# Three steps moved in the hand-written order of an attention and expert kernel: transposed maxima, low query parts and values

## The chip, the cores and the metric

The kernel runs on one core of a Trainium2 chip. Its time is the device time of one launch in microseconds (us). The core has five engines that run side by side, each strictly in the order of its own program: TensorE (PE, with its weight loads PEld), VectorE (DVE), ScalarE (ACT), GpSimd (POOL) and SyncE (SP), which here only issues DMAs. They wait for one another by semaphores. "The profiled execution" is one execution whose instructions were recorded; its span is the time from the first to the last recorded instruction.

## The reference

Eight batches of 128 rows with 256 columns go through one attention (8 heads of 16 rows, attending over the 256 columns) and one layer with two experts. Each has a layer norm ahead and a residual sum behind.

```python
def _L0_xcond_ref(q, k, v, k_length):
    qh = q.reshape(b, NUM_HEADS, d, lq)
    kh = k.reshape(b, NUM_HEADS, d, lk)
    vh = v.reshape(b, NUM_HEADS, d, lk)
    s = SCALE * jnp.log(k_length.astype(jnp.float32))[:, None, None, None]
    attn = jnp.einsum('bhdq,bhdk->bhqk', qh, kh)
    attn = jax.nn.softmax(s * attn, axis=-1)
    out = jnp.einsum('bhqk,bhdk->bhdq', attn, vh)
    return out.reshape(b, hd, lq)
...
h = jnp.einsum('nd,ehd->enh', x_flat, w_fc)
a = jnp.square(jnp.where(h >= 0, h, 0.5 * h))
expert_out = jnp.einsum('enh,edh->end', a, w_proj)
mask = (top_idx[None, :] == jnp.arange(num_experts)[:, None]).astype(x.dtype)
out = jnp.einsum('end,en->nd', expert_out, mask * top_weight[None, :])
...
x = x + _L0_xcond_ref(_layernorm(x, axis=-1), ctx_2048, ctx_2048, itok_B_779_1933)
x = x + _L0_ffn_ref(_layernorm(x, axis=-1), L0_ffn_w_router, L0_ffn_w_fc, L0_ffn_w_proj)
```

## The kernel before

Everything stays on the chip between input and output. A batch b goes through the attention alone; two batches together form a group g for the experts. Operands of the matmuls are held as a high part and a low part (q_hi and q_lo, k_hi and k_lo, and so on for the weights), the low part being the value less the high part. For queries, ScalarE makes the high part (q_part_hi) and VectorE the low one (q_part_lo, line 698). For keys, ScalarE makes the high part (k_part_hi) and GpSimd the low one (split_k, line 301).

The steps of one batch, by the names of the helpers:

- SP stacks the parts of keys and queries by six DMAs (stack_k, stack_q, lines 161 and 169) into k_st and q_st, of which there are two each, for even and odd batches. The stacks of batch b may be overwritten once all four scores_kq of batch b-2 are done.
- scores_qk(b, g), line 1141, g from 0 to 3: PE's score products for a pair of heads, from which only the row maxima are taken. The first of a batch waits for all six stacking DMAs. In batches 0 and 1 they alternate between the PSUM tiles snp and hp; from batch 2 on all go to snp, so scores_qk(b, g) also waits for row_max(b, g-1).
- row_max(b, g), line 721: VectorE's maximum over a row, negated, into negm. split_max_hi(b) and split_max_lo(b), lines 729 and 734, make the two parts nm_r of it.
- max_transpose(b), line 1156: PE transposes nm_r into snp. ScalarE copies it to mx (max_rows, line 428).
- scores_kq(b, g), lines 1171 and 1175: the scores again, transposed, with the maximum already taken off, into stp (in batch 1 into hp for even g). The first of a batch waits for mx.
- exp(b, g), line 435: ScalarE's exponential into the tile probs of pair g. It overwrites what values(b-1, 0) reads for g = 0 and 1, and what values(b-1, 1) reads for g = 2 and 3, and waits for them.
- values(b, 0) and values(b, 1), line 1191: PE's 16 matmuls each over the pairs 0 and 1, and 2 and 3, into the two halves of the PSUM tile pv.
- pv_turn(b), line 740, waits for both halves. Behind it on VectorE come den_inverse (744), attention_out (749, the division), attention_turn (755, the second transpose), x2_sum (761, the residual sum) and the statistics x2_moments (660, 663, 666).

Each pair of batches then goes through x_transpose, ffn1 (line 1213), leaky and square steps and ffn2 (line 1231). The weights of the experts come in 16 pieces by DMA and are split into parts by ScalarE with GpSimd (split_w, line 312) or VectorE. fill(n), line 1148, and warm are matmuls on a zero tile that nobody reads.

No scheduler sets the order. Each engine's program is a list of such calls, written out by hand, and the change edits two of the five lists: VectorE's and PE's.

Of the kernel before, what the change touches and what calls it, by code (L numbers as in the profile page):

```python
# [24 lines left out]
def build(nc, x, ctx_kv, ctx_t, w_router, w_fc_t, w_proj_t, consts, out):  # L25
# [3 lines left out]
    with ExitStack() as stack:  # L29
# [100 lines left out]
        def wait(eng, s, value):  # L130

            if value > 0:
                eng.wait_ge(s, value)
# [523 lines left out]
        def _(dve):  # L657
# [25 lines left out]
            def x_newton(b, stage):  # L683
                j = b % 2
                newton(stage, b, xvar[j], xrs[j], xn1[j], xsc[j], s_xrs, s_xn1, s_xsc)
# [8 lines left out]
            def q_part_lo(b):  # L694
                j = b % 2
                dve.wait_ge(s_qhi, b + 1)
                wait(dve, s_qst[j], 48 * (b // 2))
                dve.tensor_tensor(q_lo[j][:, :], q_f[j][:, :], q_hi[j][:, :].bitcast(f32), ALU.subtract).then_inc(s_qlo, 1)
# [19 lines left out]
            def row_max(b, g):  # L718
                pair = hp if b < 2 and g % 2 == 1 else snp
                dve.wait_ge(s_sn, PAIRS * b + g + 1)  # L720
                dve.tensor_reduce(negm[b % 2][:, :, :, g].rearrange("p c e -> p e c"),  # L721
                                  pair[:, :, :].rearrange("p e (c n) -> p e c n", c=KC),
                                  AX.X, ALU.max, negate=True).then_inc(s_max, 1)
# [160 lines left out]
            row_max(1, 0)  # L884
            row_max(1, 1)
            row_max(1, 2)
            row_max(1, 3)
            x_newton(3, 0)
            x_moments(4, 0)
# [2 lines left out]
            split_max_lo(1)  # L892
            x_moments(4, 2)
            x_newton(3, 1)
            q_part_lo(2)
            x_newton(4, 0)
            q_normalise(3)
            x_newton(4, 1)
# [230 lines left out]
        def _(pe):  # L1129
            def scores_qk(b, g):  # L1130
                j = b % 2
                pair, sets = (hp if b < 2 and g % 2 == 1 else snp), (2 if b < 2 else 1)
                if g == 0:
                    pe.wait_ge(s_qst[j], 48 * (b // 2) + 48)
                    pe.wait_ge(s_kst[j], 48 * (b // 2) + 48)
                    wait(pe, s_mrows, b)
                wait(pe, s_max, PAIRS * b + (g - sets + 1))
                for qc in range(KC):
                    for e in range(2):
                        rows = slice(HALF * e, HALF * e + HALF)  # L1140
                        last = pe.matmul(pair[:, e, qc * KEYS:(qc + 1) * KEYS], q_st[j][rows, g, qc * P:(qc + 1) * P],  # L1141
                                         k_st[j][rows, g, :], start=(qc == 0), stop=True, skip_group_check=True)
                last.then_inc(s_sn, 1)

            def fill(n):

                for _ in range(n):
                    pe.matmul(ops_[:, 0:P], blank[:, 0:P], blank[:, 0:P], start=True, stop=True, skip_group_check=True)

            def max_transpose(b):  # L1150
                j = b % 2
                pe.wait_ge(s_nmlo, b + 1)
                if b == 0:
                    pe.wait_ge(s_cst, 16)
                for qc in range(KC):
                    last = pe.transpose(snp[:, 0, qc * P:(qc + 1) * P],
                                        nm_r[j][:, qc, :, :].rearrange("p e r -> p (e r)").bitcast(f32), ident)
                last.then_inc(s_mt, 1)

            def scores_kq(b, g):  # L1160
                j = b % 2
                if g == 0:
                    pe.wait_ge(s_mrows, b + 1)
                    if b == 0:
                        pe.wait_ge(s_picks, 1)
                pair = hp if b == 1 and g % 2 == 0 else stp
                wait(pe, s_exp, PAIRS * b + g - (1 if b == 1 and g > 0 else 0))
                for kc in range(KC):
                    for e in range(2):
                        rows = slice(HALF * e, HALF * e + HALF)  # L1170
                        pe.matmul(pair[:, e, kc * DIM:(kc + 1) * DIM], k_st[j][rows, g, kc * P:(kc + 1) * P], q_st[j][rows, g, :],  # L1171
                                  start=(kc == 0), stop=False, skip_group_check=True)
                    for e in range(2):
                        rows = slice(HALF * e, HALF * e + HALF)
                        last = pe.matmul(pair[:, e, kc * DIM:(kc + 1) * DIM], pick[rows, g, :], mx[j][rows, :],  # L1175
                                         start=False, stop=True, skip_group_check=True)
                last.then_inc(s_st, 1)

            def values(b, e):
                j = b % 2  # L1180
                pe.wait_ge(s_exp, PAIRS * b + PAIRS // 2 * (e + 1))
                if e == 0:
                    pe.wait_ge(s_vone, b + 1)
                    if b == 0:
                        pe.wait_ge(s_vones, 2)
                    wait(pe, s_pvt, b)
                    wait(pe, s_xtlo, b // 2)
                for kc in range(KC):
                    for g in range(PAIRS):
                        h = PAIRS * e + g  # L1190
                        last = pe.matmul(pv[32 * g:32 * g + 32, e * DIM:(e + 1) * DIM], v_one[j][:, kc * HEADS + h, :],  # L1191
                                         probs[h // 2][:, h % 2, kc, :], start=(e == 0 and kc == 0), stop=(e == 1 and kc == KC - 1),
                                         skip_group_check=True)
                last.then_inc(s_pv, 1)
# [75 lines left out]
            scores_qk(1, 3)  # L1270
            fill(2)
            scores_kq(0, 3)
            values(0, 0)
            max_transpose(1)
            values(0, 1)
            scores_kq(1, 0)
            scores_kq(1, 1)
            scores_qk(2, 0)
            scores_kq(1, 2)
            values(1, 0)  # L1280
# [233 lines left out]
```

## Time and profile before

| what | us |
|---|---|
| median of 3 runs | 178.3 |
| lowest and highest run | 178.22, 179.01 |
| the profiled execution's own time | 178.59 |
| its span | 176.8 |
| PE busy (matmuls) | 160.6 |
| VectorE busy | 125.6 |
| ScalarE busy | 95.4 |
| GpSimd busy | 57.9 |

The profiled execution's time is 1.8 us above its span, and 0.3 us above the median. Busy times of different engines lie beside one another and don't add up to the span. The timelines below give, for each instruction or run of like instructions, its start in us from the beginning of the span and its duration; a bracket behind a row tells how long the engine stood idle before it, and what ended that.

### The profile page before, as it was taken

The numbers are of one execution on the slowest core, as the hardware profiler recorded it, in microseconds if no ns is written. First come the engines' busy times: TensorE is split into PE (matmuls) and PEld (weight loads), VectorE is DVE, ScalarE is ACT, GpSimd is POOL, SyncE is SP. The second block draws the span as 40 slices with busy tenths as digits, with TensorE's granted clock in tenths as the row PEclk, the third lists the DMA queues.
The fourth block names the chain that finished last, engine by engine and source line by source line (L and its number), as shares of the span: only waits on it lengthen the run. The fifth ranks groups of instructions, "written<-read, shape, count | busy, mean of one in ns | idle before, by whom it ended". The sixth has DMA issues, their size and how long they took to land.

```text
span 176.8 us, 4088 instructions
## 1 busy us (share of the span) xinstructions
PE 160.6 (91%) x1516; PEld 139.6 (79%) x1516; DVE 125.6 (71%) x298; ACT 95.4 (54%) x179; POOL 57.9 (33%) x66
## 2 busy tenths in 40 slices
PE   2987795858999999999999999999999999999990
PEld 2866653546698968869898899969879999999990
DVE  6778879988997887799969937669238449345311
ACT  4432868946566749773559353644782463434400
POOL 7232805600044922133344241202241606343310
PEclk9999999999999999999999999999999999999999
DMA  4887856672356045024000460000010000010001
GB/s 134 266 287 232 267 193 212 215 235 65 124 154 200 4 140 186 6 75 132 4 2 30 153 178 0 4 0 6 0 36 27 0 0 0 4 59 0 4 0 59
DMA packets 18355, 16.32 MB, mean 92 GB/s; under 512 B 1696, under 2 KB 18208, under 8 KB 18336
## 3 DMA queue, kind: packets, MB, share of 16 engines
q1 hardware_dynamic: 17472, 15.21, 26.9%
q10 hardware_dynamic: 864, 0.86, 1.7%
q8 instruction: 12, 0.20, 0.5%
q14 instruction: 7, 0.06, 0.1%
HBM read 8.72 MB, written 1.05 MB: 55 GB/s over the span
## 4 chain that ended last, share of the span: by engine, by line
PE 73%; DMA 7%; DVE 6%; SPq 5%; ACT 4%; issue 3%; ACTq 0%; DVEq 0%
PE ops L1231 27%; PE hp L1213 24%; PE pv L1191 6%; PE stp L1171 6%; PE snp L1141 4%; DMA q_st<-q_lo 4%; PE stp L1175 4%; DVE negm L721 3%; ACT probs L435 3%; SPq L161 2%; DMA x_raw<-x 2%; DMA q_st<-q_hi 2%; SPq L169 1%; DVE wproj_lo L841 1%; PE pv L1241 1%
## 5 line engine op out<-in xcount | busy, mean ns | idle before, releaser
L319 POOL TENSOR_TENSOR a_buf<-l_buf 128x512 f32<-128x512 f32 x32 | 35.1, 1101 | 85.6 <-ACT l_buf L443 64.0
L435 ACT ACTIVATE probs<-stp,scale_b 128x1024 f32<-128x1024 f32 x30 | 33.4, 1114 | 21.5 <-PE stp L1175 21.2
L721 DVE TENSOR_REDUCE negm<-snp 128x4 f32<-128x1024 f32 x28 | 34.2, 1223 | 13.9 <-PE snp L1141 13.6
L1213 PE MATMUL hp<-xt_hi,wfc_hi 128*128 128x256 f32 x128 | 37.5, 293 | 0.0
L1213 PE MATMUL hp<-xt_hi,wfc_lo 128*128 128x256 f32 x128 | 35.8, 279 | 0.0
L1213 PE MATMUL hp<-xt_lo,wfc_hi 128*128 128x256 f32 x128 | 35.8, 279 | 0.0
L819 DVE TENSOR_TENSOR a_lo<-a_buf,a_hi 128x512 fp32r<-128x512 f32 x32 | 23.5, 745 | 12.7 <-ACT a_hi L450 8.1
L443 ACT ACTIVATE l_buf<-hp 128x512 f32<-128x512 f32 x32 | 18.8, 593 | 17.8 <-PE hp L1213 17.8
L1231 PE MATMUL ops<-wproj_hi,a_hi 128*128 128x256 f32 x128 | 27.0, 292 | 0.0
L1213 PEld LDWEIGHTS hp<-xt_hi,wfc_hi 128*128 128x128 f32 x128 | 24.1, 188 | 2.9 <-issue 1.6
L1231 PE MATMUL ops<-wproj_hi,a_lo 128*128 128x256 f32 x128 | 25.6, 281 | 0.0
L1231 PE MATMUL ops<-wproj_lo,a_hi 128*128 128x256 f32 x128 | 25.5, 281 | 0.0
L1213 PEld LDWEIGHTS hp<-xt_hi,wfc_lo 128*128 128x128 f32 x128 | 24.1, 188 | 0.0
L1213 PEld LDWEIGHTS hp<-xt_lo,wfc_hi 128*128 128x128 f32 x128 | 24.1, 188 | 0.0
L450 ACT ACTIVATE a_hi<-l_buf 128x512 fp32r<-128x512 f32 x32 | 19.7, 625 | 3.8 <-PE ops L1231 3.7
L1231 PEld LDWEIGHTS ops<-wproj_hi,a_hi 128*128 128x128 f32 x128 | 19.5, 188 | 1.7 <-issue 0.4
L1171 PE MATMUL stp<-q_st,k_st 64*128 64x256 f32 x120 | 17.6, 313 | 3.1 <-ACT probs L435 2.1
L1231 PEld LDWEIGHTS ops<-wproj_lo,a_hi 128*128 128x128 f32 x128 | 19.6, 188 | 0.0
L1231 PEld LDWEIGHTS ops<-wproj_hi,a_lo 128*128 128x128 f32 x128 | 19.6, 188 | 0.0
L1141 PE MATMUL snp<-k_st,q_st 64*128 64x256 f32 x112 | 12.9, 309 | 4.4 <-DMA q_st<-q_lo 3.2
L1191 PE MATMUL pv<-probs,v_one 128*32 128x256 f32 x256 | 16.2, 384 | 0.3 <-DVE xt_lo L846 0.3
L1171 PEld LDWEIGHTS stp<-q_st,k_st 64*128 64x128 f32 x120 | 11.2, 184 | 6.3 <-ACT probs L435 3.1
(81 smaller groups left out, 224.9 us busy)
## 6 DMA issues: line engine op xcount, KB each, us to landing
k_st<-k_hi SPq DMA_DIRECT2D x16, 128.0 KB, 2.5
wfc_raw<-w_fc_t SPq DMA_DIRECT2D x8, 256.0 KB, 3.6
wproj_raw<-w_proj_t SPq DMA_DIRECT2D x8, 256.0 KB, 3.2
q_st<-q_hi SPq DMA_DIRECT2D x14, 128.0 KB, 2.4
x_raw<-x SPq DMA_DIRECT2D x8, 128.0 KB, 2.6
v_raw<-ctx_t SPq DMA_DIRECT2D x8, 128.0 KB, 2.8
k_st<-k_lo SPq DMA_DIRECT2D x8, 128.0 KB, 2.5
q_st<-q_lo SPq DMA_DIRECT2D x8, 128.0 KB, 2.3
```

What stands on the lines that cost most here:

```text
L319: pool.tensor_tensor(a_buf[d % 2][:, :, :], l_buf[d % 2][:, :, :], l_buf[d % 2][:, :, :], ALU.mult).then_inc(s_a, 1)
L435: act.activation(probs[g][:, :, :, :], (hp if b == 1 and g % 2 == 0 else stp)[:, :, :].rearrange("p e (c n) -> p e c n", c=KC), ACT.Exp, s ...
L443: act.activation(l_buf[d % 2][:, :, :], hp[:, d % 2, :].rearrange("p (c n) -> p c n", c=2), ACT.Prelu, alpha=0.5).then_inc(s_l, 1)
L450: act.activation(a_hi[d % NA][:, :, :], l_buf[d % 2][:, :, :], ACT.Square).then_inc(s_ahi, 1)
L721: dve.tensor_reduce(negm[b % 2][:, :, :, g].rearrange("p c e -> p e c"), pair[:, :, :].rearrange("p e (c n) -> p e c n", c=KC), AX.X, ALU. ...
L819: dve.tensor_tensor(a_lo[d % NA][:, :, :], a_buf[d % 2][:, :, :], a_hi[d % NA][:, :, :].bitcast(f32), ALU.subtract).then_inc(s_alo, 1)
L1141: last = pe.matmul(pair[:, e, qc * KEYS:(qc + 1) * KEYS], q_st[j][rows, g, qc * P:(qc + 1) * P], k_st[j][rows, g, :], start=(qc == 0), sto ...
L1171: pe.matmul(pair[:, e, kc * DIM:(kc + 1) * DIM], k_st[j][rows, g, kc * P:(kc + 1) * P], q_st[j][rows, g, :], start=(kc == 0), stop=False, ...
L1175: last = pe.matmul(pair[:, e, kc * DIM:(kc + 1) * DIM], pick[rows, g, :], mx[j][rows, :], start=False, stop=True, skip_group_check=True)
L1191: last = pe.matmul(pv[32 * g:32 * g + 32, e * DIM:(e + 1) * DIM], v_one[j][:, kc * HEADS + h, :], probs[h // 2][:, h % 2, kc, :], start=(e ...
L1213: last = pe.matmul(hp[:, d % 2, half], wfc[w][:, kc, c * P:(c + 1) * P], xt[:, kc, :], start=(c % 2 == 0 and kc == 0 and w == 0 and xt is ...
L1231: last = pe.matmul(ops_[:, t * DIM:(t + 1) * DIM], a[d % NA][:, c % 2, t * P:(t + 1) * P], wproj[w][:, c, :], start=(c % CH == 0 and part ...
```

## The change

```diff
@@ -884,6 +884,7 @@
             row_max(1, 0)
             row_max(1, 1)
             row_max(1, 2)
+            q_part_lo(2)
             row_max(1, 3)
...
             split_max_lo(1)
             x_moments(4, 2)
             x_newton(3, 1)
-            q_part_lo(2)
             x_newton(4, 0)
@@ -1270,11 +1270,11 @@
             scores_kq(0, 3)
+            max_transpose(1)
             values(0, 0)
-            max_transpose(1)
-            values(0, 1)
             scores_kq(1, 0)
             scores_kq(1, 1)
+            values(0, 1)
             scores_qk(2, 0)
```

On VectorE, the low query parts of batch 2 are made ahead of the last maximum of batch 1 instead of seven rows behind it. On PE, the transposed maxima of batch 1 go ahead of the first half of batch 0's values, and the second half of these values goes behind the first two transposed score products of batch 1. No instruction is added or removed, and the programs of ScalarE, GpSimd and SP are as before.

PE's order before, from the end of scores_kq(0, 3) to the first score product of batch 2; pv is the tile of the values, the row into snp from nm_r is max_transpose(1), hp and stp take scores_kq(1, 0) and (1, 1):

```order
L1175 MATMUL stp<-mx,pick 128x256 x2
L1191 MATMUL pv<-probs,v_one 32x256 x8
L1156 MATMUL snp<-cst,nm_r 128x128 x2
L1191 MATMUL pv<-probs,v_one 32x256 x8
L1171 MATMUL hp<-q_st,k_st 128x256 x2
L1175 MATMUL hp<-mx,pick 128x256 x2
...
L1171 MATMUL stp<-q_st,k_st 128x256 x2
L1175 MATMUL stp<-mx,pick 128x256 x2
L1141 MATMUL snp<-k_st,q_st 128x256 x4
```

The same stretch in the changed kernel:

```order
L1175 MATMUL stp<-mx,pick 128x256 x2
L1156 MATMUL snp<-cst,nm_r 128x128 x2
L1191 MATMUL pv<-probs,v_one 32x256 x8
L1171 MATMUL hp<-q_st,k_st 128x256 x2
L1175 MATMUL hp<-mx,pick 128x256 x2
...
L1171 MATMUL stp<-q_st,k_st 128x256 x2
L1175 MATMUL stp<-mx,pick 128x256 x2
L1191 MATMUL pv<-probs,v_one 32x256 x8
L1141 MATMUL snp<-k_st,q_st 128x256 x4
```

The transposes have passed the first half of the values, and the second half now stands directly ahead of batch 2's first score product.

VectorE's order in the changed kernel as a difference to before, with buffer numbers; negm1 takes batch 1's maxima and q_lo0 batch 2's low query parts:

```order
 L721 TENSOR_REDUCE negm1<-hp 128x2x2
 L721 TENSOR_REDUCE negm1<-snp 128x2x2
+L698 TENSOR_TENSOR q_lo0<-q_f0,q_hi0 128x256
 L721 TENSOR_REDUCE negm1<-hp 128x2x2
 L672 SCALAR_TENSOR_TENSOR xn11<-xrs1,xvar1 128x1
...
 L666 TENSOR_SCALAR xvar0<-xmv0 128x1
 L675 SCALAR_TENSOR_TENSOR xsc1<-xn11,xrs1 128x1
-L698 TENSOR_TENSOR q_lo0<-q_f0,q_hi0 128x256
 L672 SCALAR_TENSOR_TENSOR xn10<-xrs0,xvar0 128x1
 L691 TENSOR_SCALAR q_f1<-x_raw1,xmv1,xsc1 128x256
```

The subtraction has passed row_max(1, 3), the two split steps of the maxima and four small statistics.

What follows on VectorE stands in the same order before and after, from pv_turn(0), which reads pv, to row_max(2, 0), which reads snp:

```order
L740 STREAM_TRANSPOSE pvt<-pv 128x512
L744 RECIPROCAL den_r<-pvt 128x16
L749 TENSOR_TENSOR att_t<-pvt,den_r 128x2x128
L755 STREAM_TRANSPOSE att<-att_t 128x256
L698 TENSOR_TENSOR q_lo1<-q_f1,q_hi1 128x256
L761 TENSOR_TENSOR x2_0<-x_keep0,att 128x256
L660 BN_STATS yst0<-x2_0 128x6
L663 BN_AGGR ymv0<-yst0 128x2
L721 TENSOR_REDUCE negm0<-snp 128x2x2
```

Nothing in this chain was moved; its first step waits for values(0, 1), which was.

## Rows read from the trace of the kernel before

**Rows 1.** The page, part 1: busy us (share of the span) xinstructions.

```profile
PE 160.6 (91%) x1516; PEld 139.6 (79%) x1516; DVE 125.6 (71%) x298; ACT 95.4 (54%) x179; POOL 57.9 (33%) x66
```

**Rows 2.** PE's waits, 53 to 177 us: us in total, times, longest.

```profile
PE snp L1141 <- DMA q_st<-q_lo: 0.2, 1, 0.2
```

**Rows 3.** PE's timeline, 20 to 34 us: start, duration, what, [idle before].

```profile
23.37 1.07 PE L1191 MATMUL pv<-probs,v_one 128*32 128x256 f32 x16
24.37 0.44 PE L1156 MATMUL snp<-cst,nm_r 128*128 128x128 f32 x2
24.74 1.07 PE L1191 MATMUL pv<-probs,v_one 128*32 128x256 f32 x16
25.74 0.39 PE L1171 MATMUL hp<-q_st,k_st 64*128 64x256 f32 x2
...
26.68 0.28 PE L1175 MATMUL stp<-mx,pick 64*128 64x256 f32 x2
28.97 0.51 PE L1141 MATMUL snp<-k_st,q_st 64*128 64x256 f32 x4 [2.01 <-DMA q_st<-q_lo]
...
30.87 0.50 PE L1141 MATMUL snp<-k_st,q_st 64*128 64x256 f32 x4
```

**Rows 4.** The timeline of SP's DMA issues, 20 to 34 us.

```profile
24.93 0.54 SPq L161 DMA_DIRECT2D k_st<-k_hi  x1
...
26.86 0.55 SPq L169 DMA_DIRECT2D q_st<-q_lo  x1
...
32.63 1.47 SPq L161 DMA_DIRECT2D k_st<-k_hi  x1
```

**Rows 5.** ScalarE's timeline, 20 to 34 us.

```profile
20.90 0.41 ACT L402 ACTIVATE q_hi<-q_f 128x256 fp32r<-128x256 f32 x1
...
24.85 0.38 ACT L428 ACTIVATE mx<-snp 128x256 fp32r<-128x256 f32 x1
...
27.85 0.42 ACT L396 ACTIVATE k_hi<-kv_raw 128x256 fp32r<-128x256 f32 x1
```

**Rows 6.** VectorE's timeline, 20 to 34 us.

```profile
21.77 1.23 DVE L721 TENSOR_REDUCE negm<-hp 128x4 f32<-128x1024 f32 x1 [0.40 <-PE hp L1141]
...
23.59 0.15 DVE L734 TENSOR_TENSOR nm_r<-negm,nm_r 128x16 fp32r<-128x16 f32 x1
...
25.88 0.72 DVE L740 STREAM_TRANSPOSE pvt<-pv 128x512 f32<-128x512 f32 x1 [0.31 <-PE pv L1191]
...
26.92 0.43 DVE L749 TENSOR_TENSOR att_t<-pvt,den_r 128x256 f32<-128x256 f32 x1
27.38 0.45 DVE L755 STREAM_TRANSPOSE att<-att_t 128x256 f32<-128x256 f32 x1
27.98 0.42 DVE L698 TENSOR_TENSOR q_lo<-q_f,q_hi 128x256 fp32r<-128x256 f32 x1 [0.15 <-ACT q_hi L402]
...
29.23 0.18 DVE L663 BATCH_NORM_AGGREGATE ymv<-yst 128x2 f32<-128x6 f32 x1
29.52 1.23 DVE L721 TENSOR_REDUCE negm<-snp 128x4 f32<-128x1024 f32 x1
```

**Rows 7.** GpSimd's timeline, 20 to 34 us.

```profile
21.08 0.74 POOL L301 TENSOR_TENSOR k_lo<-kv_raw,k_hi 128x256 fp32r<-128x256 f32 x1
28.34 0.98 POOL L301 TENSOR_TENSOR k_lo<-kv_raw,k_hi 128x256 fp32r<-128x256 f32 x1 [6.53 <-ACT k_hi L396]
29.29 1.28 POOL L312 TENSOR_TENSOR wfc_lo<-wfc_raw,wfc_hi 128x512 fp32r<-128x512 f32 x1
```

**Rows 8.** VectorE's timeline, 93 to 97 us.

```profile
95.32 0.76 DVE L698 TENSOR_TENSOR q_lo<-q_f,q_hi 128x256 fp32r<-128x256 f32 x1
```

**Rows 9.** GpSimd's timeline, 93 to 97 us.

```profile
94.75 1.04 POOL L319 TENSOR_TENSOR a_buf<-l_buf 128x512 f32<-128x512 f32 x1 [2.86 <-ACT l_buf L443]
95.75 0.92 POOL L301 TENSOR_TENSOR k_lo<-kv_raw,k_hi 128x256 fp32r<-128x256 f32 x1
```

**Rows 10.** DMAs issued 24.9 to 25.0 us: KB, us from issue to landing.

```profile
k_st<-k_hi SPq DMA_DIRECT2D x1, 128.0 KB, 2.8
```

## The prediction

> **What bounds the kernel now.** I read the page's busy shares, then PE's waits by stretch, then the timelines of all engines between 20 and 34 us. The page says that PE is busy for 91% of the span, and that VectorE (DVE) comes next at 71% [rows 1]. PE's waits over the last 124 us, from 53 us on, are one wait of 0.2 us [rows 2]. So from 53 us PE works without a pause, and a delay of PE before that point is a delay of the end: nothing later can take it up. All three moved pieces lie between 21 and 26 us, in the stage in which PE still waits. There the reader is to look at two waits of PE. The first score product of batch 2, scores_qk(2, 0), starts at 28.97 after 2.01 us of idle time, released by a DMA (the low query parts of batch 2). The next one, scores_qk(2, 1), starts at 30.87, right behind the values of batch 1 [rows 3].
>
> The 28.97 is fixed from elsewhere. SP's queue issues six stacking DMAs for batch 2, one after another, the third at 24.93 and the last at 26.86 [rows 4]. They may start only when scores_kq(0, 3) is done, which the change doesn't move, and the last of them lands about 2.1 us after its issue. Anything on PE between 23.4 and 28.97 can be reordered without moving that product. What can move is the work behind it that VectorE has to do in time.
>
> **Part 1, the low query parts of batch 2 ahead of a maximum.** q_part_lo(2) needs the high parts, which ScalarE has ready at 20.90 + 0.41 = 21.31 [rows 5]. VectorE is idle for 0.40 us before row_max(1, 3), which starts at 21.77 [rows 6]. The piece takes 0.42 (as q_part_lo(3) does at 27.98, same rows), so it would run from 21.33 to 21.75 and cost nothing. But GpSimd runs k_lo, a subtraction of two SBUF tiles, from 21.08 to 21.82 [rows 7]. Late in the kernel the same meeting is on record: q_lo started at 95.32, 0.57 us into a GpSimd operation of 1.04 us from 94.75, and took 0.76 in place of 0.42. It ended 0.29 after that operation's end, and the GpSimd operation behind it took 0.92 in place of 0.74 [rows 8, 9]. By that, q_part_lo(2) ends at 21.82 + 0.29 = 22.11 and row_max(1, 3) starts some 0.25 us late. I take 0.25, with 0 as the other end. What this piece brings is nothing: its DMA stands last in SP's series and goes at 26.86, long after either time.
>
> **Part 2, the transposed maxima ahead of values(0, 0).** Before, max_transpose(1) starts at 24.37, after 1.00 us of values work that began at 23.37 [rows 3]. After, it waits for split_max_lo(1), whose last step was done at 23.59 + 0.15 = 23.74 [rows 6] and is now done at about 24.0. The transposes start at 24.05, and values(0, 0) at 24.05 + 0.37 = 24.42, with its next work 1.00 later, at 25.42. ScalarE copies the maxima at 24.85 in either case, since it comes from exp(0, 3) and two small steps that end then [rows 5]; the copy is done at 25.23. So scores_kq(1, 0) starts at 25.42 in place of 25.74. This is a gain of 0.3 us for exp(1, 0), and of 0.5 without the 0.25 of part 1. It is lost again: exp(1, 2) has to wait for a product that stands behind scores_qk(2, 0) at 28.97 on PE.
>
> **Part 3, values(0, 1) behind two score products.** It started at 24.74 and now starts after scores_kq(1, 0) and (1, 1), whose matmuls run from 25.74 to the last pair at 26.68 [rows 3]. Other work can start about 0.2 behind that pair, so they hold PE for 1.15, and 25.42 + 1.15 = 26.57. It ends at 27.64 in place of 25.81. On PE that is still free, since PE then idles until 28.97. On VectorE it isn't. pv_turn(0), the transpose that reads both halves of the values, started at 25.88, right behind them [rows 6], and now starts at 27.71, 1.83 later. Behind it, in program order, stand the inverse, the division (26.92), the second transpose (27.38), q_part_lo(3) (27.98), x2_sum(0), two moment steps (the last at 29.23, 0.18 long, so done at 29.41), and only then row_max(2, 0) at 29.52. The last of these frees the score bank for scores_qk(2, 1). Before, this chain ended 0.1 us before the scores came: the slack is used up.
>
> Without any meeting with GpSimd: VectorE is free for q_part_lo(3) 1.95 us after pv_turn started (27.38 + 0.45 - 25.88), at 29.66 (or 29.48 without the 0.25 of part 1). From q_lo's start to the end of the moments it takes 29.41 - 27.98 = 1.43, so row_max(2, 0) starts at about 31.0, ends at 32.2, and scores_qk(2, 1) starts at 32.25 in place of 30.87. That is 1.4 late, or 1.2 without the 0.25. I call this 1.3.
>
> **What the shifted chain runs into.** GpSimd runs k_lo(4) at 28.34 and right behind it a weight split of 1.28 us from 29.29 [rows 7]. Before, VectorE was done with its operations on two SBUF tiles when the split began, and only k_lo(4) was touched (0.98, where k_lo at 21.08 took 0.74). These don't move with the change: k_lo(4) waits for ScalarE's k_hi(4) at 27.85 [rows 5], and that needs the batch-2 stacking DMA issued at 24.93, which lands 2.8 us later, at 27.7 [rows 4, 10]. So GpSimd now holds 28.34 to 29.08 and, behind it, 1.28 us more. VectorE comes to the division at 27.71 + 1.04 = 28.75, inside k_lo(4), and ends it at 29.08 + 0.29 = 29.37. Its second transpose goes to 29.83. Meanwhile the weight split has begun, held up by 0.18 as in [rows 9], and ends at 29.05 + 1.28 + 0.18 = 30.5. q_part_lo(3) reaches the engine at 29.74 and ends 0.29 after the split, at 30.8. The rest of the chain takes 29.41 - 28.40 = 1.01, so row_max(2, 0) starts at about 31.8, ends at 33.0, and scores_qk(2, 1) starts at 33.0: 33.0 - 30.87 = **2.1 us late**. The 0.25 of part 1 drops out here, because GpSimd's end sets the time.
>
> The Trainium skill (SBUF — State Buffer, section "Who interferes with whom") says that a VectorE instruction with two SBUF inputs and a GpSimd instruction that reads SBUF exclude each other for a whole instruction, and whichever was issued first holds the ports. The trace agrees where it shows the meeting, with 0.76 in place of 0.42 [rows 8]. By this rule the delay is the 2.1; if it did not hold for the pairs met here, it would be the 1.3.
>
> **Does the delay travel?** scores_kq(1, 3) stands right behind scores_qk(2, 1), and its end releases batch 3's stacking DMAs, whose landing releases scores_qk(3, 0). The other maxima of batch 2 follow one another through PE and VectorE, each product behind the maximum before it. Both paths shift whole. The one thing that could give back is SP's issue at 32.63, which took 1.47 where its like took 0.54 to 0.59 [rows 4]. If the stall behind that is over by the time SP comes there, up to 0.9 is regained on the DMA path, though the path by the exponentials would keep most of the delay. I take 0 and keep 0.9 for the range.
>
> **The sum.** Part 1 gives 0, part 2 gives 0, and part 3 costs 2.1, of which 1.3 is program order and 0.8 is the meeting with GpSimd. The profiled execution took 178.59 with a span of 176.8, so it would take 180.7. The median of the runs is 178.3, 0.3 lower, and on it I predict **180.4 us**, 1.2% more.
>
> **The rivals.**
> First, GpSimd costs nothing, because the division or q_part_lo(3) slips ahead of the weight split: 1.3 late, 179.6. For it speaks that single times here are within 0.1 to 0.2 us of each other; against it, that q_part_lo(3) falls into the middle of a 1.28 us operation. Chance 0.17.
> Second, the delay is made up before 53 us (SP's 0.9 and shorter landings once the weight loads are through): 0 to 0.6 late, 178.3 to 178.9. Against it speak the waits on maxima and on exponentials that shift as well. Chance 0.09.
> Third, faster: the 0.3 to 0.5 us by which scores_kq(1, 0) comes earlier is handed on, 177.8. It would need the chain behind pv_turn(0) to be done by 29.52, that is, values(0, 1) done by about 25.9, or VectorE to need less than the 3.53 us that it took from 25.88 to 29.41. Work that was back to back has no such room. Chance 0.04.
> Fourth, still slower: another meeting with GpSimd, whose weight splits go on, or a DMA stall that now falls worse. Over 181.0, chance 0.10.
> The forecast itself, 1.6 to 2.6 late, has 0.60.
>
> **How the numbers follow.** Leaving out the second and third rival and the fourth leaves out 0.23. To come under 0.2 the range goes from 179.2 (the first rival with some of SP's 0.9 given back) to 181.1. A measurement of this kernel can tell about 0.5%, 0.9 us, from no change. Slower by more than that are the forecast, the fourth rival and nearly all of the first: 0.85. Within it are most of the second and a little of the first: 0.11. Faster: 0.04.
>
> **What would show it.** In the profile after, scores_qk(2, 0) should stand at about 29.0 as before, scores_kq(1, 0) at 25.2 to 25.5, pv_turn(0) at 27.5 to 27.7, q_part_lo(3) at 29.5 to 29.8 with a duration near 1.0, row_max(2, 0) at 31.8, and scores_qk(2, 1) at 33.0 after an idle time of about 2 us that a maximum ends. q_part_lo(2) should take about 0.75. Batch 3's first product should be 1.2 to 2.1 later. I am wrong if scores_qk(2, 0) moves, if q_part_lo(3) takes 0.42, or if PE's start on the first expert product isn't later by what scores_qk(2, 1) was.

## The result, and the profile after

The changed kernel took 182.1 us (median of 4 runs, 181.7 to 183.9), the kernel before 178.6 beside it. The ratio is 1.018, with a 95% interval of 1.013 to 1.024. The sign was right; the size was forecast at 2.1 us and is 3.5, and 182.1 lies above the predicted range of 179.2 to 181.1. Ratios here and below leave out runs that lie more than 1.5% above the fastest of their kernel. The profiled execution took 182.02 with a span of 180.2, 3.4 more than before. Each run also lists TensorE's mean granted clock as a share of full speed. Here it was 0.966 to 0.991 and never full, and that will matter.

The page's parts 1 and 2 of the kernel after (PEclk is the granted clock of 40 slices, in tenths):

```profile
PE 162.9 (90%) x1516; PEld 140.7 (78%) x1516; DVE 126.8 (70%) x298; ACT 95.4 (53%) x179; POOL 57.7 (32%) x66
PEclk9999999969999999999999999999999999999998
```

The same 1516 matmuls are busy for 2.3 us longer than in [rows 1], and one slice, 36.0 to 40.6 us, has a 6 where before had 9 throughout. So TensorE waited longer and, for a moment, also worked slower.

PE's waits of the kernel after, 20 to 36 us (us in total, times, longest):

```profile
PE snp L1141 <- DVE negm L721: 2.5, 2, 2.3
PE snp L1141 <- DMA q_st<-q_lo: 1.3, 1, 1.3
```

The timeline of PE, same kernel (start, duration, what, idle before and its releaser), with max_transpose(1), the moved values(0, 1), scores_qk(2, 0) and scores_qk(2, 1). It answers to [rows 3]:

```profile
24.26 0.44 PE L1156 MATMUL snp<-cst,nm_r 128*128 128x128 f32 x2 [0.58 <-DVE nm_r L734]
...
25.63 0.39 PE L1171 MATMUL hp<-q_st,k_st 64*128 64x256 f32 x2
...
26.79 1.07 PE L1191 MATMUL pv<-probs,v_one 128*32 128x256 f32 x16
29.16 0.50 PE L1141 MATMUL snp<-k_st,q_st 64*128 64x256 f32 x4 [1.30 <-DMA q_st<-q_lo]
...
33.43 0.51 PE L1141 MATMUL snp<-k_st,q_st 64*128 64x256 f32 x4 [2.30 <-DVE negm L721]
```

The new wait is the one that was forecast: scores_qk(2, 1) idles 2.30 us for a maximum and starts at 33.43. All records of this execution lie about 0.2 later from 21 us on (scores_qk(2, 0) too), so net of that it is 2.4 late.

The timelines of VectorE and GpSimd, same kernel. They answer to [rows 6, 7]: q_part_lo(2), then the chain from pv_turn(0) to row_max(2, 0), then GpSimd's k_lo(4) and the weight split:

```profile
21.57 0.76 DVE L698 TENSOR_TENSOR q_lo<-q_f,q_hi 128x256 fp32r<-128x256 f32 x1
...
27.93 0.72 DVE L740 STREAM_TRANSPOSE pvt<-pv 128x512 f32<-128x512 f32 x1 [2.12 <-PE pv L1191]
28.68 0.25 DVE L744 RECIPROCAL den_r<-pvt 128x16 f32<-128x16 f32 x1
28.96 1.51 DVE L749 TENSOR_TENSOR att_t<-pvt,den_r 128x256 f32<-128x256 f32 x1
30.50 0.45 DVE L755 STREAM_TRANSPOSE att<-att_t 128x256 f32<-128x256 f32 x1
30.87 0.38 DVE L698 TENSOR_TENSOR q_lo<-q_f,q_hi 128x256 fp32r<-128x256 f32 x1
...
32.19 1.19 DVE L721 TENSOR_REDUCE negm<-snp 128x4 f32<-128x1024 f32 x1
```

```profile
28.22 0.72 POOL L301 TENSOR_TENSOR k_lo<-kv_raw,k_hi 128x256 fp32r<-128x256 f32 x1 [6.17 <-ACT k_hi L396]
28.90 1.28 POOL L312 TENSOR_TENSOR wfc_lo<-wfc_raw,wfc_hi 128x512 fp32r<-128x512 f32 x1
```

The meeting with GpSimd is there, in another place. The division comes at 28.96, just behind the end of k_lo(4) (28.22 + 0.72 = 28.94) and 0.06 us into the weight split, and waits for the split's end: 28.90 + 1.28 + 0.29 = 30.47, where it ends. It takes 1.51 in place of the 0.43 or so that it takes undisturbed, and q_part_lo(3) finds the way free with 0.38. The forecast had the division come inside k_lo(4). But k_lo(4) starts at 28.22 in place of 28.34, which is 0.3 earlier net of the 0.2: on ScalarE, exp(1, 0) starts at 26.42 in place of 26.52, and k_hi(4) follows it.

The windows of the kernel after (busy us of PE, PEld, DVE, ACT, POOL with counts, then the granted clock, DMA share, GB/s):

```profile
32.00:33.00 1.00, 0.00 (x0) 0.00 (x0) 0.97 (x3) 0.00 (x0) 1.00 (x1) 1.00 0.32 102
...
35.00:36.00 1.00, 0.80 (x9) 0.52 (x12) 0.48 (x5) 1.00 (x4) 0.00 (x0) 0.70 0.23 75
36.00:37.00 1.00, 1.00 (x12) 0.48 (x16) 1.00 (x1) 1.00 (x3) 0.44 (x1) 0.50 0.24 65
37.00:38.00 1.00, 1.00 (x10) 0.25 (x4) 0.34 (x2) 1.00 (x4) 0.83 (x1) 0.50 0.61 204
38.00:39.00 1.00, 1.00 (x7) 0.78 (x8) 1.00 (x2) 0.32 (x3) 0.00 (x0) 0.59 0.67 211
```

This is the other cost. TensorE does nothing from 31.13 to 33.43 and then works at the full clock (2.4 GHz) until about 35.4. From there to about 38.8 it has half of it (1.2 GHz), and then the full one again. Before, the windows from 33 to 39 us all show 1.00. The Trainium skill (TensorE: Matmul & The Clock Gate, section "Part 1: The HAM clock gate") says that the clock follows how busy TensorE has been shortly before; the trace agrees in that the half clock follows the idle time, though it doesn't come in it.

The work in the stretch at half the clock is on the way to the end. PE's timeline, the kernel before and then the kernel after: values(1, 1), max_transpose(2), scores_qk(3, 0), and the first expert product:

```profile
33.12 1.07 PE L1191 MATMUL pv<-probs,v_one 128*32 128x256 f32 x16
...
36.76 0.44 PE L1156 MATMUL snp<-cst,nm_r 128*128 128x128 f32 x2 [0.43 <-DVE nm_r L734]
...
39.79 0.50 PE L1141 MATMUL snp<-k_st,q_st 64*128 64x256 f32 x4 [0.96 <-DMA q_st<-q_lo]
...
47.52 0.39 PE L1213 MATMUL hp<-xt_hi,wfc_hi 128*128 128x256 f32 x1
```

```profile
35.88 1.93 PE L1191 MATMUL pv<-probs,v_one 128*32 128x256 f32 x16
...
40.29 0.44 PE L1156 MATMUL snp<-cst,nm_r 128*128 128x128 f32 x2 [0.28 <-DVE nm_r L734]
...
42.29 0.50 PE L1141 MATMUL snp<-k_st,q_st 64*128 64x256 f32 x4
...
50.66 0.39 PE L1213 MATMUL hp<-xt_hi,wfc_hi 128*128 128x256 f32 x1
```

values(1, 1) takes 1.93 in place of 1.07. As a sum of what the traces show:

| start of | before | after | later | of it |
|---|---|---|---|---|
| scores_qk(2, 0) | 28.97 | 29.16 | 0.2 | start of the trace |
| scores_qk(2, 1) | 30.87 | 33.43 | 2.6 | 2.4 for the maximum |
| max_transpose(2) | 36.76 | 40.29 | 3.5 | 1.0 more at half the clock |
| scores_qk(3, 0) | 39.79 | 42.29 | 2.5 | its DMA was waited for 0.96 before, 0 now |
| scores_kq(2, 1) | 40.13 | 43.15 | 3.0 | waits for an exponential of batch 2 |
| first expert product | 47.52 | 50.66 | 3.1 | |
| scores_qk(4, 0) | 53.16 | 56.60 | 3.4 | its DMA was waited for 0.24 before, 0.55 now |

Batch 3's first product gives 1.0 back, but the chain of batch 2 (maximum, transposed maximum, exponential) gives back only 0.5, and the end follows that one. The last 0.3 comes at batch 4's first product. PE's rows before and after, and SP's issue ahead of it in the kernel after, where the same issue before took 1.57:

```profile
53.16 0.50 PE L1141 MATMUL snp<-k_st,q_st 64*128 64x256 f32 x4 [0.24 <-DMA q_st<-q_lo]
```

```profile
56.60 0.51 PE L1141 MATMUL snp<-k_st,q_st 64*128 64x256 f32 x4 [0.55 <-DMA q_st<-q_lo]
```

```profile
51.07 1.80 SPq L177 DMA_DIRECT2D v_raw<-ctx_t  x1
```

From 57 us on PE doesn't wait at all.

### The profile page after: what moved, and what is told of

Read it like the earlier page. It is cut to its first block, busy times and chain, and to the rows that moved or that the text cites. A ratio compares the mean times of both kernels' runs of the same rounds, so it can differ in the third digit from the quotient of the medians.

```text
span 180.2 us, 4088 instructions
## 1 busy us (share of the span) xinstructions
PE 162.9 (90%) x1516; PEld 140.7 (78%) x1516; DVE 126.8 (70%) x298; ACT 95.4 (53%) x179; POOL 57.7 (32%) x66
## 3 DMA queue, kind: packets, MB, share of 16 engines
q1 hardware_dynamic: 17472, 15.21, 26.5%
HBM read 8.72 MB, written 1.05 MB: 54 GB/s over the span
## 4 chain that ended last, share of the span: by engine, by line
PE 77%; DVE 12%; issue 4%; ACT 4%; DMA 1%; DVEq 0%; ACTq 0%
PE ops L1231 26%; PE hp L1213 24%; PE pv L1191 8%; PE stp L1171 6%; DVE negm L721 5%; PE snp L1141 4%; PE ops L1200 4%; PE stp L1175 3%; ACT probs L435 2%; DMA q_st<-q_lo 1%; PE snp L1156 1%; DVE wproj_lo L841 1%; DVE q_st L713 1%; PE pv L1241 1%; DVE att_t L749 1%
## 5 line engine op out<-in xcount | busy, mean ns | idle before, releaser
L450 ACT ACTIVATE a_hi<-l_buf 128x512 fp32r<-128x512 f32 x32 | 19.7, 625 | 3.8 <-PE ops L1231 3.7
L1191 PE MATMUL pv<-probs,v_one 128*32 128x256 f32 x256 | 17.1, 399 | 0.3 <-DVE xt_lo L846 0.3
```

Of the source, the lines that this page charges most:

```text
L450: act.activation(a_hi[d % NA][:, :, :], l_buf[d % 2][:, :, :], ACT.Square).then_inc(s_ahi, 1)
```

## The experiments

My theory after the result had three parts. (a) values(0, 1) behind the score products carries the whole loss. (b) Of it, 1.3 is program order on VectorE and about 1 the meeting with GpSimd. (c) The idle time of TensorE brings a stretch at half the clock, worth about 1.3 more. The rivals: the moved query parts delay everything (against a), and the rest comes from a DMA or maximum path and not from the clock (against c). In what follows "at the full clock" means runs whose mean granted clock was 0.995 or more. There the kernel before took 178.5 to 179.0 (medians of 6, 8 and 6 such runs on three chips, of 55 in all).

**PE's two moves without the query parts.** The changed kernel, with q_part_lo(2) back in its place.

```diff
             row_max(1, 2)
-            q_part_lo(2)
             row_max(1, 3)
```

> The two moves on PE alone (transposed maxima ahead of values(0, 0), values(0, 1) behind two score products); VectorE's order as before. Theory: all of the loss is PE's two moves, by three terms that follow one another: the chain on VectorE behind values(0, 1), the division that waits for GpSimd, and half the TensorE clock after PE's long idle time. Then scores_qk(2, 1) stands at 33.2 to 33.5 as in the changed kernel and the time is 181.7 to 182.3. Rival: the low query parts ahead of the maximum, which took 0.76 in place of 0.42 there, carry a good part of it; then this is under 181.2.

Measured: 183.2 to 184.4 (4 runs), ratio 1.026 [1.021, 1.031]. The loss stays, so the query parts don't cause it. It is larger than I expected, because the clock was also at half from 20 to 26 us in the profiled execution, before any of the moves could act. The profiled executions of the next two experiments, which carry no loss, show the same early fall; the one profile of the kernel before doesn't. The three lines are the window, the division and scores_qk(2, 1):

```profile
24.00:26.00 2.00, 2.00 (x12) 1.56 (x11) 2.00 (x9) 1.03 (x2) 0.00 (x0) 0.50 0.44 141
```

```profile
31.23 1.52 DVE L749 TENSOR_TENSOR att_t<-pvt,den_r 128x256 f32<-128x256 f32 x1
```

```profile
35.72 0.50 PE L1141 MATMUL snp<-k_st,q_st 64*128 64x256 f32 x4 [2.17 <-DVE negm L721]
```

**The query parts alone.** The kernel before, with q_part_lo(2) ahead of row_max(1, 3) and nothing else.

> The low query parts of batch 2 ahead of row_max(1, 3) alone, PE's order as before. Theory: q_part_lo(2) takes 0.76 beside GpSimd's subtraction and row_max(1, 3) starts 0.25 late, but the transposed maxima stand behind values(0, 0) on PE until 24.4 anyway: 178.3 to 178.9, no difference. Rival: it costs by itself what it delays, 0.3 us, or sets off something later: 179.2 or more.

Measured: 178.5 to 179.1 in the four runs at the full clock, ratio 1.0025 [0.997, 1.008]. No difference; its own duration was 0.76, as in the changed kernel. The profiled execution (182.4) has the early fall, and a second one behind the 1.91 us that PE waits for the low query parts: half the clock from 33.2 to 36.6. So the wait that the kernel before has already can be followed by one too.

**The transposed maxima alone.** The kernel before with max_transpose(1) ahead of values(0, 0), and values(0, 1) behind it as before.

```diff
+            max_transpose(1)
             values(0, 0)
-            max_transpose(1)
             values(0, 1)
```

> The kernel before with one edit: the transposed maxima of batch 1 ahead of both halves of batch 0's values, which stay together; the low query parts stay. Theory: harmless. The transposes wait 0.4 us, values(0, 1) ends within 0.4 us of where it did (26.0 to 26.2), row_max(2, 0) within 0.4 of 29.5, and runs at full clock take 178.3 to 178.9. Rival, that the transposes' wait is part of the loss: 179.2 or more at full clock.

Measured: 178.1 to 179.2 in the six runs at the full clock, 0.996 [0.992, 1.000]. Harmless.

**The values alone.** The kernel before with only values(0, 1) moved.

```diff
-            values(0, 1)
             scores_kq(1, 0)
             scores_kq(1, 1)
+            values(0, 1)
             scores_qk(2, 0)
```

> The kernel before with one edit: values(0, 1) behind scores_kq(1, 0) and (1, 1); the transposed maxima stay between the two halves of the values, the low query parts stay where they were. Theory: this one move carries the loss. values(0, 1) is done about 1.2 us later than before and the division meets GpSimd's k_lo(4) and weight split as in the changed kernel: scores_qk(2, 1) at 32.5 to 33.5, time 181 to 182.5. Rival, that the loss needs the transposes ahead too: under 180.

Measured: 181.4 to 182.3 (4 runs, clock 0.987 to 0.991), 1.014 [1.008, 1.020]. This one line is the loss. The division, scores_qk(2, 1), what PE waits for before the clock falls, and the window of the fall:

```profile
28.93 1.50 DVE L749 TENSOR_TENSOR att_t<-pvt,den_r 128x256 f32<-128x256 f32 x1
```

```profile
33.40 0.50 PE L1141 MATMUL snp<-k_st,q_st 64*128 64x256 f32 x4 [2.19 <-DVE negm L721]
```

```profile
39.30 0.44 PE L1156 MATMUL snp<-cst,nm_r 128*128 128x128 f32 x2 [0.43 <-DVE nm_r L734]
40.21 0.39 PE L1171 MATMUL stp<-q_st,k_st 64*128 64x256 f32 x2 [0.47 <-ACT mx L428]
...
41.90 0.50 PE L1141 MATMUL snp<-k_st,q_st 64*128 64x256 f32 x4 [0.53 <-DMA q_st<-q_lo]
```

```profile
42.00:44.00 2.00, 2.00 (x16) 1.78 (x17) 1.56 (x3) 1.25 (x4) 0.40 (x1) 0.63 0.51 142
```

Here the clock stays full until about 42.5 and falls then, 9 us behind the end of the wait. Right ahead of this fall TensorE had three short idle times, 0.43, 0.47 and 0.53. The kernel before has the same ones at 36.3 to 39.8 (0.43, 0.47, 0.96) and keeps the full clock behind them in its profile. So this trace doesn't tell which idle time the fall belongs to.

**The gap filled.** TensorE's idle time before scores_qk(2, 1) is filled with products of a blank tile that nobody reads (fill, which the kernel has in other gaps already).

```diff
             values(1, 0)
+            fill(16)
             scores_qk(2, 1)
```

> The changed kernel with 16 matmuls on the zero tile between values(1, 0) and scores_qk(2, 1), about 1.9 us of work that nobody reads, in PE's idle time of 2.3. Nothing is left out. Theory: scores_qk(2, 1) stays at 33.4, the granted clock stays full between 35 and 40 us, where it is at half in the changed kernel, and the time is 0.8 to 1.2 lower: 180.9 to 181.3. Rival, that the clock falls for another reason or costs nothing: 182.0 to 182.3, half clock still seen.

Measured: 183.2 median, ratio 1.023 [1.014, 1.032], and 182.0 and 182.1 in the two runs at the full clock. I had the size of a fill wrong: fill(16) is 32 matmuls and takes 3.84 us.

```profile
31.16 3.84 PE L1148 MATMUL ops<-blank 128*128 128x128 f32 x32
34.93 0.50 PE L1141 MATMUL snp<-k_st,q_st 64*128 64x256 f32 x4
```

That makes scores_qk(2, 1) some 1.4 later than it need be. Repeated with fill(9), 2.27 us:

> The changed kernel with 9 fill steps (18 matmuls on the zero tile, 2.2 us) between values(1, 0) and scores_qk(2, 1), so that they fit PE's idle time of 2.3 (16 such steps took 3.84 us and were too many). Nothing is left out. Theory: scores_qk(2, 1) stays at 33.4, the clock stays full from 35 to 40 us, and runs whose clock is at 0.995 or more take 180.7 to 181.2, against 181.7 to 182.2 for the changed kernel. Rival, that the half clock there has nothing to do with the idle time: it is seen between 35 and 39 us all the same and the time is 181.7 or more.

Measured: five of ten runs at the full clock, and these took 180.5 to 180.7; the others 181.7 to 183.9, down to a clock of 0.966 (ratio 1.011 [1.006, 1.016]). I had expected 180.7 to 181.2 at the full clock. The distance between scores_qk(2, 0) and (2, 1) is 4.13 in this trace and 4.27 in that of the changed kernel, so the fill delays nothing. The wait is as long as before, only busy: I take 180.6 for the changed kernel without its half clock. Its stretch behind the gap, with the clock full:

```profile
36.00:38.00 2.00, 1.75 (x20) 1.41 (x20) 1.90 (x6) 1.17 (x2) 0.02 (x1) 1.00 0.49 144
```

**The same fill without the query parts** (the first experiment with fill(9)):

> PE's two moves alone, the low query parts where they were, with 9 fill steps ahead of scores_qk(2, 1). Nothing is left out. Theory: the low query parts ahead of the maximum cost nothing beside PE's moves, since GpSimd's split sets the time: runs at full clock take 180.3 to 180.7, as the changed kernel does with the same fill steps. Rival, that they cost their 0.25 us: 180.1 to 180.3. A third, that they matter more: under 180.

Measured: 180.4 to 180.7 in the five of ten runs at the full clock; ratio 1.012 [1.008, 1.017]. That is 0.2 below the runs with them, but on another chip, and between these two chips the kernel before differs by 0.5 (178.5 and 179.0). Whether the query parts cost 0 or their 0.25 isn't shown.

**The maximum first.** The changed kernel with row_max(2, 0) directly behind den_inverse(0), ahead of the division and all that follows.

```diff
             den_inverse(0)
+            row_max(2, 0)
             attention_out(0)
...
             x2_moments(0, 1)
-            row_max(2, 0)
```

> The changed kernel, with row_max(2, 0) on VectorE put directly behind the inverse, ahead of the division, second transpose, low query parts, residual sum and moments. Nothing is left out. Theory: scores_qk(2, 1) waits for VectorE's program order; row_max(2, 0) then runs at 29.7 (right behind the scores), scores_qk(2, 1) starts at 31.0 to 31.2, PE's idle time ahead of it is gone, and the time is that of the kernel before within 0.8 us: 178.4 to 179.5 where the clock stays full. Rival, that the late end of the values costs by another way (a tile that comes free late, a DMA): 180.5 or more.

Measured: 183.9 median, 1.026 [1.020, 1.033]. A clear miss. scores_qk(2, 1) starts at 31.36 without a wait, as wanted, and the wait reappears one product on, longer:

```profile
31.36 0.51 PE L1141 MATMUL snp<-k_st,q_st 64*128 64x256 f32 x4
...
36.43 0.79 PE L1141 MATMUL snp<-k_st,q_st 64*128 64x256 f32 x4 [3.44 <-DVE negm L721]
```

The chain that I had moved out of the way now stands in front of row_max(2, 1), where its residual sum meets the next weight split:

```profile
32.43 1.49 DVE L761 TENSOR_TENSOR x<-x_keep,att 128x256 f32<-128x256 f32 x1
...
35.16 1.21 DVE L721 TENSOR_REDUCE negm<-snp 128x4 f32<-128x1024 f32 x1
```

VectorE has the same work to do between values(0, 1) and batch 2's second maximum, wherever the first one stands. This change of the order within it freed no time.

**The weight split out of the way.** Three tries at (b), each the changed kernel with GpSimd's split moved. First, split 3 ahead of k_lo(4):

```diff
             split_k(3)
-            split_k(4)
             split_w(0, 3)
+            split_k(4)
```

> The changed kernel, with GpSimd's fourth weight split put ahead of its k_lo(4) (it can run from 23.2 us on, where GpSimd is idle). Nothing is left out. This takes the operation away into which VectorE's division runs. Theory: the division takes 0.43 in place of 1.51, scores_qk(2, 1) starts 1.1 earlier, at about 32.3, PE's idle time ahead of it is 1.2 and the clock stays full: 179.6 to 180.2. If the clock falls all the same: 180.6 to 181.2. Rival, that GpSimd isn't the cause of the 1.51: 182.

Measured: 183.0 median, 1.013 [1.006, 1.020]. The division took 0.43, but the moved split now met the steps that prepare the transposed maxima (a cast took 1.16), and in the profiled execution the clock fell three times, at 19.7, 26.5 and 36.7. Not conclusive. With a fill(4) before scores_qk(2, 1):

> The changed kernel with GpSimd's fourth weight split ahead of k_lo(4), so that the division no longer meets it, and 4 fill steps (1 us) ahead of scores_qk(2, 1) for the clock. Nothing is left out. Theory: the division takes 0.43, scores_qk(2, 1) starts at 32.2 to 32.5 and what is left is the cost of program order alone, 1.3 us: 179.6 to 180.2 where the clock stays full. Rival, that GpSimd's part was small: 180.7 or more.

Measured: 181.7 median, 1.012 [1.002, 1.021]; 180.4 and 180.7 at the full clock. No gain over 180.6, against what I expected. The rows of VectorE and GpSimd show why:

```profile
23.74 1.28 POOL L312 TENSOR_TENSOR wfc_lo<-wfc_raw,wfc_hi 128x512 fp32r<-128x512 f32 x1 [1.43 <-ACT wfc_hi L463]
24.14 0.91 DVE L729 CAST nm_r<-negm 128x16 fp32r<-128x16 f32 x1
```

A cast of 16 columns takes 0.91 in place of 0.15. What the division saves, the transposed maxima lose. Last, the split later instead: GpSimd holds split 3 until ScalarE has the next piece's high parts.

```diff
-                pool.wait_ge(s_whi[w], n + 1)
+                pool.wait_ge(s_whi[w], n + 2 if w == 0 and n == 3 else n + 1)
```

> The changed kernel with GpSimd's fourth weight split made to wait for the high parts of the fifth piece, so that it starts at about 31.8, behind VectorE's operations with two SBUF inputs, and 4 fill steps ahead of scores_qk(2, 1). Nothing is left out. Theory: the division takes 0.43, scores_qk(2, 1) starts at 32.2 to 32.4 in place of 33.4, and runs at full clock take 179.3 to 179.9, against 180.5 to 180.7 for the changed kernel with its idle time filled. Rival, that GpSimd's hold on the division isn't worth 1 us to the end: 180.3 or more.

Measured: 179.95 and 181.17 at the full clock, both above what I expected; median 181.7, 1.011 [1.004, 1.018]. In the trace the first half of (b) stands bare: the division undisturbed, and scores_qk(2, 1) 3.22 behind scores_qk(2, 0), where it was 1.90 [rows 3]. The 1.32 is program order alone.

```profile
28.89 0.42 DVE L749 TENSOR_TENSOR att_t<-pvt,den_r 128x256 f32<-128x256 f32 x1
```

```profile
29.06 0.50 PE L1141 MATMUL snp<-k_st,q_st 64*128 64x256 f32 x4 [1.28 <-DMA q_st<-q_lo]
...
32.28 0.50 PE L1141 MATMUL snp<-k_st,q_st 64*128 64x256 f32 x4 [0.16 <-DVE negm L721]
...
34.72 0.50 PE L1141 MATMUL snp<-k_st,q_st 64*128 64x256 f32 x4 [0.82 <-DVE negm L721]
```

But the late splits, two in a row, then held a piece of batch 4's queries for 1.06 in place of 0.41, and scores_qk(2, 2) waited for it with 0.82. A meeting was moved again, not removed. In this trace the clock is at half from 42 to 48 us, in spite of the fill.

**Fills for the kernel before.** If idle time costs clock, the kernel before should gain as well where it waits. It gets 11 more fills: one more behind scores_qk(0, 3), one behind max_transpose(0), two ahead of scores_kq(0, 1), and seven ahead of scores_qk(2, 0):

```diff
             scores_kq(1, 1)
+            fill(7)
             scores_qk(2, 0)
```

> The kernel before with matmuls on the zero tile in PE's idle times: 2 fill steps more around the transposes of batch 0, 2 ahead of scores_kq(0, 1), 7 ahead of scores_qk(2, 0). Nothing is left out. Theory: the best runs stay where they are (178.3 to 178.6), and fewer runs show a clock under 0.99, which 5 and 4 of 13 runs of the kernel before did: the median falls by 0.3 to 0.8 us. Rival, that these falls of the clock don't come from idle times of PE that can be filled: the same share of runs is disturbed, median within 0.2 us.

Measured: 178.55 median of 12 runs (178.22 to 179.59), ten of them at the full clock. On the same chip the kernel before took 180.2 in the median of 29 runs (178.3 to 183.8), six at the full clock; the ratio is 0.996 [0.993, 0.999]. The best runs of both are alike: the fills make nothing faster, they keep the clock. PE's wait for the low query parts went from 2.0 [rows 3] to 0.2, as fill work:

```profile
27.14 1.83 PE L1148 MATMUL ops<-blank 128*128 128x128 f32 x14
29.16 0.51 PE L1141 MATMUL snp<-k_st,q_st 64*128 64x256 f32 x4 [0.20 <-DMA q_st<-q_lo]
```

**What the clock costs, over all runs.**

| kernels | runs at the full clock |
|---|---|
| changed, and the variants with the 2 to 3 us wait left idle (5 kernels) | 0 of 20 |
| the variants with that wait filled (5 kernels) | 16 of 32 |
| before | 20 of 55 |
| before, with the fills | 10 of 12 |

The limit of 0.995 is mine. With 0.994 the last column reads 0, 16, 26 and 11: six runs of the kernel before at 0.994 took 178.3 to 179.1, as the full ones did.

The best pair is the changed kernel (181.7 to 182.2 in three of its runs) and the one with fill(9) at the full clock (180.6). By it the half clock costs 1.1 to 1.6, though the two weren't run side by side. The 55 runs of the kernel before agree: on a straight line through them, 0.01 less of the mean clock goes with 1.16 us more, which makes 1.0 to 2.2 for the 0.991 to 0.981 of those three runs (an estimate). The rest, 180.6 less the 178.5 of the kernel before on the same chip, is 2.1. On the chip of the second run with fill(9), which leaves the query parts where they were, it is 180.4 less 179.0, or 1.4.

Not all of the 1.1 to 1.6 need be the clock's. Between the profiles of the changed kernel and of that second filled one (spans of 180.2 and 178.6), 0.9 arises between scores_qk(2, 1) and the first expert product, and about 0.6 at batch 4's first product, which waits 0.55 in one and not at all in the other. That wait is seen in the seven profiles in which SP's issue ahead of it took 1.57 to 1.80, the kernel before among them, and in none of the others. Whether the clock has to do with this issue wasn't tested.

## Why the prediction was right in sign and too low

**What bounds the kernel, and that part 3 alone counts:** right. scores_qk(2, 0) starts at 29.16 (28.97 plus the shift of the whole trace), and the experiments that make part 1 or part 2 alone show no loss, while the one with values(0, 1) alone shows it.

**Part 1:** q_part_lo(2) takes 0.76, and row_max(1, 3) is late by the meeting with k_lo. I had this drop out of the end; the runs don't decide it, as said at the second run with fill(9).

**Part 2:** max_transpose(1) at 24.26 and scores_kq(1, 0) at 25.63 are, less the 0.2 of the trace, the forecast 24.05 and 25.42. What I missed is that the gain reaches GpSimd: with exp(1, 0) and k_hi(4), k_lo(4) and the split came 0.3 earlier, though I had written that these don't move.

**Part 3, program order, 1.3:** measured alone as 1.32, with the split held back.

**The meeting with GpSimd, 0.8:** 1.05 in the trace (2.37 less 1.32). I had the division meet k_lo(4) and get in ahead of the split, ending at 29.37, and q_part_lo(3) be the one that waits. It was the other way round: the split had begun when the division came, and the division waited. One of my own signs of being wrong is thereby met, q_part_lo(3) without a wait (0.38). That the sum came out near all the same is in part luck, since two errors offset one another. VectorE was free again at 30.47, or 30.27 less the 0.2 of the trace, 0.5 before the forecast 30.8. But behind that point stood 1.72 us of work up to row_max(2, 0), with the second transpose and q_part_lo(3) in it, and not the forecast 1.01. The Trainium skill (SBUF — State Buffer, "Who interferes with whom"), by which the whole-instruction exclusion gave 2.1, was nearer than the rival by which the meeting costs nothing.

**Does the delay travel?** Nearly as said. scores_qk(3, 0) gave back 1.0, because its DMA had been waited for before; the path by the exponentials gave back 0.5, and that one sets the end. SP's long issue hardly helped: it is the same issue, batch 3's first of k_st, and took 0.2 less. The timeline of SP's issues, kernel after, answers to the 1.47 of [rows 4]:

```profile
35.20 1.25 SPq L161 DMA_DIRECT2D k_st<-k_hi  x1
```

**The sum is the step that failed.** It added up part 3 and the meeting and nothing else. It had a price for what PE waits and none for the clock at which PE works afterwards. I read PEclk in the page before, saw 9 throughout, and took that as a property of the kernel. It was one of the outcomes of a kernel that waits much between 14 and 29 us: 35 of its 55 runs weren't at the full clock (29 with the limit at 0.994), though the runs that I had (178.2 to 179.0) showed little of it. What the runs show in place of that zero is 1.1 to 1.6 us, of which the traces place 0.9 in the stretch up to the first expert product. No row of the kernel before had a stretch at half the clock, so the size couldn't be read there; but a new idle time of 2 us on TensorE just before a dense stretch called for a term and a wider range. Without that term the sum comes near: 180.6 measured against 180.4 on one chip, with a loss of 2.1 there and of 1.4 on another. A second, smaller term stood at nothing: I had PE's waits from 53 us on stay as they were, and the 0.2 there became 0.5.

**The rivals.** The first three are out. The fourth (over 181.0) had the right side and the wrong mechanism: the half clock made most of the difference, not a second meeting with GpSimd. A DMA wait has at most the 0.3 at batch 4's first product.

**What stays open:** what sets the moment of the fall. In the changed kernel it came 2.0 behind the end of the long wait, in PE's two moves alone and in the early split 0.5 behind it, and with the maximum first 0.3 ahead of its end. With values(0, 1) alone and with the late split it came only at 42.5 and 41.4, amid short idle times of 0.36 to 0.53. The filled variants and the kernel before still lose clock in half of their runs or more; five of the profiled executions here have a fall between 19 and 26 us, which I tested only through the fills in the kernel before. That the fills work by the clock is concluded from runs and windows together; no run changed the clock alone.

## What to carry to other kernels

Moving a step later in a hand-written order is paid for by what stands behind its reader on the other engine: find the reader, follow that engine's program to the step that frees the next bank, and compare with when the bank is wanted. Where the slack there is 0.1 us, no order within the chain helps, and moving the neighbour that it meets only moves the meeting. A wait of 2 us or more on TensorE can have a second price, the clock of a stretch behind it, in more runs or fewer; here, filling gaps with products that nobody reads lowered that price without making the best run faster. So such a change is to be judged over many runs.

## What the runs showed of the hardware

- A VectorE operation with two SBUF inputs that comes while a GpSimd operation runs waits for that operation's end, and ends 0.29 behind it (128x256): the division, which began about 0.06 us into a split, took 1.50 to 1.52 in six kernels, 0.42 or 0.43 without the meeting. It waits for the one operation only: with the maximum first, the residual sum ended 0.28 behind a split (32.18 + 1.46), and it was GpSimd's next operation, from 33.59, that took 0.59 in place of 0.40.
- Not only operations with two tiles are held. A cast of 128x16 took 0.91 in place of 0.15, and a tensor_scalar of 128x256 took 1.06 in place of 0.41 (ending at 33.20, behind the first of two splits in a row, which ended at 33.05). The Trainium skill (SBUF — State Buffer, "Who interferes with whom") names cast and tensor_scalar among the operations that can contend and tensor_reduce as one that never does on this chip; the rows agree, since the maxima (TENSOR_REDUCE), which here read PSUM, took 1.19 to 1.23 throughout.
- TensorE at half the clock takes 1.93 us for a group of 16 matmuls of the values, against 1.07. A kernel with one such stretch of 3.4 us took 1.1 to 1.6 us of 180 longer, 0.9 of it in and right behind the stretch. It began 2.0 us behind the end of a wait of 2.30 in one trace, and 0.3 ahead of the end of a wait of 3.44 in another.
- SP's long issue (1.47 before, 1.25 after, of the same DMA) isn't bound to one DMA: in the second kernel with fill(9), whose SP program is the same, the issue at 32.06 of a weight load took 1.43.
